# A quarter of a gate softmax moved from matrix products to broadcast rows on three other engines

## The chip, the cores and the metric

One core of a Trainium2 chip runs the whole program; the metric is device time in microseconds, lower is better. The engines are TensorE (PE in the profile, PEld for its weight loads), VectorE (DVE), ScalarE (ACT), GpSimd (POOL) and SyncE (SP), which issues the plain DMAs.

## The reference

Input `x` is (16, 64, 64, 256) in float32: 16 images of 4096 pixels with 256 channels. Four residual layers follow each other, each on the group-normalized (`_gn`) input. Layer 0 adds the nearest of 1024 code vectors, layer 1 an attention of sigmoid scores over rows of 64 pixels, layer 3 a linear attention with a channel norm. The change is in layer 2, a gate from a rank-one softmax over all pairs of pixels of an image:

```python
x = x + _L0_conv_ref(_gn(x), L0_conv_embeddings)      # argmin over 1024 codes, take
x = x + _L1_conv_ref(_gn(x), L1_conv_Wf, ...)
x = x + _L2_conv_ref(_gn(x), L2_conv_w1, ...)
x = x + _L3_conv_ref(_gn(x), L3_conv_w_qkv, ...)

def _L2_conv_ref(x, w1, b1, w2, b2, w3, b3):          # xf: (16, 4096, 256)
    x0 = jnp.einsum('bnc,c->bn', xf, w1) + b1[0]
    x1 = jnp.einsum('bnc,c->bn', xf, w2) + b2[0]
    x2 = jnp.einsum('bnc,c->bn', xf, w3) + b3[0]
    sim = x0[:, :, None] * x1[:, None, :]
    sm = jax.nn.softmax(sim, axis=1)
    feats = jnp.einsum('bn,bnm->bm', x2, sm)
    gate = jax.nn.sigmoid(feats).reshape(b, h, w, 1)
    return gate * x
```

For each column m of 4096 the gate is thus sum over n of x2[n] exp(x0[n] x1[m] - max), divided by the sum of the exponentials alone: 16.8 million exponentials per image.

## The kernel before, in words

The order of work on every engine is written out by hand. `images(B)` runs 15 loop bodies. In one, `new` goes through layers 0 and 1 and the set-up of layer 2, `old` (the image before) through the gate softmax and most of layer 3, and `last` (the one before that) through the end of layer 3 and its output. Each engine has its own list of calls such as `fill(old, 34, 0); score(new, 0, 0)`; a call issues a few instructions with semaphore waits ahead of them. An engine runs its list strictly in order, so a call that waits holds everything behind it. Behind the loop stands a last list, where `old` is the last image and there is no `new`.

The 4096 pixels are 32 tiles of 128. Gate softmax before, on image `old`, in `HALVES = 64` steps h:

- `fill(h, z)`, two matmuls with 12 rows of contraction (x0 and x1 split into bf16 pieces, so that the products come out exact enough), writes sim minus its bound for 128 values of n and 2 x 512 values of m into two PSUM banks, z = 0 or 1. Line 1363.
- `exp(h, z)` on ScalarE: one instruction of 1024 columns, PSUM to one of three SBUF buffers E. Line 601.
- `sums(h)`: four float32 matmuls, each recorded as two, with weights x2 and ones, add the numerators and denominators into PSUM bank 4 over all steps. Line 1372.
- `gate_chain`: the sums are copied, turned by TensorE, divided on VectorE, put through the sigmoid; `spread` and `gating` apply them.

Beside it on the lists stand: `final_z`, `final_sq` and `final_out` (the finish of `last`), `turn_in` (the input of `new` is transposed by TensorE, copied by VectorE), `score(new, t, half)` (six matmuls of 512 columns for half the codes of tile t; banks 5 and 6, one for each half), `best` and `index` (VectorE: maximum and its index, lines 867 and 873), GpSimd's `index` (the indexed load of code rows), `turn0` and `add0` (transpose and add), `l0_norm` and `l1_norm` (ScalarE scales, GpSimd subtracts for the low half), and layers 1 and 3.

The set-up of layer 2 (`project`, `columns`, `extremes`, `pieces`, `piece_turn`) makes x0, x1 and x2 of `new`: as rows in `rows3`, and turned, pixel on the partition, in `s3`.

SBUF is nearly full, so buffers have several uses: `work` holds the biased scores of layer 0, `soft` the q and k of layer 3 and the third E, `o_hi` also the squares of `final_sq`, `yout` the output and the gate sums.

## Time and profile before

| | |
|---|---|
| device time, median of 3 runs (lowest, highest) | 5608.44 us (5603.64, 5612.08) |
| profiled execution, first to last instruction | 5601.4 us |
| profiled execution, its own device time | not recorded; the median lies 7.0 us above its span |
| TensorE busy | 5252.2 us, 94% of the span |
| VectorE busy | 4106.3 us, 73% |
| ScalarE busy | 3978.2 us, 71% |
| GpSimd busy | 1936.0 us, 35% |
| mean granted TensorE clock | 0.966 |

Busy time is the union of an engine's instructions. Those of TensorE and ScalarE overlap at their ends, so the mean length of one is more than what it adds in a row. The granted clock is the share of TensorE's full speed. The chain that ended last follows the work back from the last instruction, at each step to what released it.

### The profile page before, as it was taken

Reading aid. Unit: us, or ns where it says so; the run is one execution under the profiler, and the core shown is the slowest. Engines: PE = TensorE matmul, PEld = TensorE weight load, DVE = VectorE, ACT = ScalarE, POOL = GpSimd, SP = SyncE. Lnnn points to the kernel's source line nnn. Section 1 sums busy time; section 2 is a strip of 40 time slices with the busy share of each in tenths; the row PEclk is TensorE's granted clock in tenths of the full one; section 3 lists DMA queues with packets and bytes.
Section 4 is the critical chain, followed back from the end, with each engine's and each line's share of the span. In section 5 each row is a group of like instructions: output and inputs, shape, how many; then the busy total and the mean of one; then the engine's idle time right before and its main releaser. Section 6 shows DMA issues by size and latency. Waiting matters only on the chain.

```text
span 5601.4 us, 113931 instructions
## 1 busy us (share of the span) xinstructions
PE 5252.2 (94%) x44520; PEld 2737.7 (49%) x44520; DVE 4106.3 (73%) x8674; ACT 3978.2 (71%) x6023; POOL 1936.0 (35%) x1594
## 2 busy tenths in 40 slices
...
GB/s 86 9 37 11 68 25 52 37 6 72 20 61 31 13 67 15 64 28 35 48 11 70 23 57 33 15 64 17 61 31 20 61 13 67 26 47 40 7 31 31
DMA packets 163253, 211.22 MB, mean 38 GB/s; under 512 B 13217, under 2 KB 146081, under 8 KB 162721
## 3 DMA queue, kind: packets, MB, share of 16 engines
...
## 4 chain that ended last, share of the span: by engine, by line
PE 66%; ACT 13%; DVE 11%; issue 6%; POOL 2%; DMA 1%; ACTq 0%; DVEq 0%; SPq 0%; POOLq 0%
PE PS L1195 33%; PE PS L1372 15%; PE PS L1363 6%; ACT n_x L529 3%; DVE stats L849 2%; PE PS L1471 2%; PE PS L1229 2%; PE PS L1253 2%; PE PS L1306 2%; ACT big L601 2%; ACT xin L529 2%; DMA quant_H<-emb_t,idx 1%; ACT work L568 1%; ACT attn L578 1%; ACT soft L601 1%
## 5 line engine op out<-in xcount | busy, mean ns | idle before, releaser
L601 ACT ACTIVATE big<-PS 128x1024 f32<-128x1024 f32 x1376 | 1365.8, 1024 | 460.3 <-PE PS L1363 398.9
L601 ACT ACTIVATE soft<-PS 128x1024 f32<-128x1024 f32 x672 | 676.2, 1024 | 353.9 <-PE PS L1363 346.3
L416 POOL DMA_INDIRECT quant_H<-emb_t,idx x512 | 487.4, 952 | 976.2 <-DVE idx L873 781.2
L1195 PE MATMUL PS<-e_hi,n_hi 128*128 128x512 f16 x2048 | 780.2, 381 | 17.3 <-DVE m L867 9.5
L1195 PE MATMUL PS<-e_hi,n_lo 128*128 128x512 f16 x2048 | 776.7, 379 | 0.0
L1195 PE MATMUL PS<-e_lo,n_hi 128*128 128x512 f16 x2048 | 776.7, 379 | 0.0
L1372 PE MATMUL PS<-big,w 128*4 128x512 f32 x5504 | 756.5, 638 | 0.0
L849 DVE BATCH_NORM_STATS2 stats<-XT 128x6 f32<-128x512 f32 x1024 | 651.7, 683 | 14.5 <-POOL XT L432 4.6
L873 DVE FIND_INDEX8 idx<-m,work 128x8 uint32<-128x1024 f32 x512 | 622.1, 1219 | 0.0
L1363 PE MATMUL PS<-rhs,lhs 12*128 12x512 bf16 x4096 | 557.6, 395 | 61.7 <-ACT big L601 38.8
L867 DVE CUSTOM_DVE_ANT_0 work<-PS,e_bias,m 128x512 f32<-128x512 f32 x512 | 384.0, 750 | 213.2 <-PE PS L1195 189.5
L867 DVE CUSTOM_DVE_ANT_0 work<-PS,e_bias 128x512 f32<-128x512 f32 x512 | 349.1, 682 | 247.1 <-PE PS L1195 239.4
L474 POOL TENSOR_TENSOR rstd<-rstd,mhalf 128x4 f32<-128x4 f32 x128 | 129.2, 1009 | 1106.1 <-DVE rstd L1054 1106.1
L1363 PEld LDWEIGHTS PS<-rhs,lhs 12*128 12x128 bf16 x4096 | 141.7, 91 | 720.2 <-ACT big L601 329.2
L529 ACT ACTIVATE n_x<-XT,gt,gs 128x512 f32<-128x512 f32 x512 | 391.9, 806 | 60.9 <-DVE gt L844 58.4
L409 POOL TENSOR_TENSOR n_lo<-n_x,n_hi 128x1024 f16<-128x1024 f32 x128 | 273.1, 2134 | 399.8 <-ACT n_hi L545 382.3
L1372 PE MATMUL PS<-soft,w 128*4 128x512 f32 x2688 | 379.0, 637 | 16.7 <-ACT soft L601 16.7
L1195 PEld LDWEIGHTS PS<-e_hi,n_hi 128*128 128x128 f16 x2048 | 199.4, 97 | 314.7 <-DVE m L867 69.4
L426 POOL TENSOR_TENSOR n_lo<-n_x,n_hi 128x1024 f16<-128x1024 f32 x128 | 273.4, 2136 | 208.4 <-ACT n_hi L559 155.4
L432 POOL TENSOR_TENSOR XT<-XT,big 128x1024 f32<-128x1024 f32 x128 | 300.2, 2367 | 90.8 <-DVE big L961 90.8
L1065 DVE SCALAR_TENSOR_TENSOR yout<-soft,rstd,PS 128x256 f32<-128x256 f32 x512 | 221.6, 475 | 139.2 <-PE PS L1471 121.1
L1195 PEld LDWEIGHTS PS<-e_hi,n_lo 128*128 128x128 f16 x2048 | 200.4, 98 | 242.2 <-issue 0.6
(208 smaller groups left out, 10799.7 us busy)
## 6 DMA issues: line engine op xcount, KB each, us to landing
xin<-x SPq DMA_DIRECT2D x128, 512.0 KB, 3.9
out<-yout SPq DMA_DIRECT2D x128, 512.0 KB, 2.9
quant_H<-emb_t,idx POOLq DMA_INDIRECT x512
XT<-emb SPq DMA_DIRECT2D x1, 1024.0 KB, 6.2
...
```

The source lines that it names most:

```text
L409: nc.gpsimd.tensor_tensor(n_lo[:, g % 2, :, :], n_x[:, g % 2, :, :], n_hi[:, g % 2, :, :], ALU.subtract).then_inc(l0_lo.sem, 1)
L416: nc.gpsimd.indirect_dma_start(quant[:, g % 2, u, :], None, emb_t, bass.IndirectOffsetOnAxis(ap=idx[:, t % (2 * GT), 0:1], axis=0),).then_ ...
L426: nc.gpsimd.tensor_tensor(n_lo[:, g % 2, :, :], n_x[:, g % 2, :, :], n_hi[:, g % 2, :, :], ALU.subtract).then_inc(l1_lo.sem, 1)
L432: nc.gpsimd.tensor_tensor(here, here, gated[:, g % 2, :, :], ALU.add).then_inc(g_added.sem, 1)
L529: return nc.scalar.activation(dst, XT[:, im % 2, k, g, :], copy, scale=gs[:, layer, k:k + 1], bias=gt[:, layer, k:k + 1])
L601: nc.scalar.activation(E[h % 3][:, z * 1024:(z + 1) * 1024], bank(2 * z, 2), ACT.Exp).then_inc(exped.sem, 1)
L849: last = v.bn_stats(stats[:, layer, k, g, :], XT[:, im % 2, k, g, :])
L867: v.tensor_tensor_reduce(biased[:, t % 2, part], bank(5 + half), e_bias[:, part], 1.0, m8[:, t % 2, 0:1] if half else -BIG, ALU.add, ALU.m ...
L873: v.max_index(idx[:, t % (2 * GT), :], m8[:, t % 2, :], biased[:, t % 2, :]).then_inc(l0_indexed.sem, 1)
L1195: ins = mm(dst, a, b, start=first and j == 0, stop=last and j == 2)
L1363: ins = mm(bank(r), lhs[rr, t * P:(t + 1) * P], rhs[rr, f * GW:(f + 1) * GW], start=True, stop=True)
L1372: ins = mm(PS[32 * q:32 * q + 4, 4, :], w2[:, t, f, :], E[h % 3][:, q * 512:(q + 1) * 512], start=h == 0, stop=h == HALVES - 1, skip_group ...
```

## The change

The 32 tiles of m are split: `NA = 24` stay on the matrix path, `NB = 8` (6 for VectorE, `KD`, and 2 for GpSimd, `KP`) leave it. The matrix path packs its 24 tiles so that each step still fills four banks, which makes 48 steps of 64.

For the other 8 tiles, m lies on the partition and n along the row. `rows_out` stores the rows x0 and x2 to DRAM, `rows_back` loads them into all 128 partitions, 2048 values of n at a time. `bexp` is one ScalarE instruction over 2048 columns, exp(x1[m] * x0[n] - max), with x1 and the negated maximum as per-partition scale and bias, and with the denominator in its accumulator; `bsum` multiplies by x2 and sums on VectorE. `pexp` does 1024 columns, and `pmul` on GpSimd multiplies by x2 and halves the length by additions until 32 are left. `gate_chain` puts the parts together. Buffers are shared anew, with waits for it, and the lists of calls are laid out anew on all engines for the steady loop and the last list. In the loop, the first `score` of `new` stands behind fill 26 (before: fill 34) on TensorE's list, the last `turn_in` behind fill 21 (before: 28).

```diff
-HALVES = 2 * NT
+KD, KP = 6, 2
+NB = KD + KP
+NA = NT - NB
+R1 = (NA - QUADS * GT) // GT
+PER = QUADS // R1
+HALVES = NT + NT // PER
...
+def strip_tiles(h):
+
+    f, i = h // NT, h % NT
+    return f, [i if f == 0 else PER * i + r // R1 for r in range(QUADS)]
...
+    rows_d = nc.dram_tensor("rows_d", (B, 2, NT * P), F32)
...
-        squares = o_hi[:, :, :, :].rearrange("p s k n -> p (s k n)").bitcast(F32).rearrange("p (u c) -> p u c", u=GT)
+        squares = sb("squares", [P, 2, C], BF16)
...
+        x0_rows = [o_both[:, :], soft[:, 0:2048]]
+        x2_rows = [n_both[:, :], o_both[:, :]]
+        EB = [work[:, :], yout[:, :, :, :].rearrange("p s u c -> p (s u c)")]
+        EP = o_x0[:, :, :].rearrange("p k n -> p (k n)")
...
+            def rows_out(im):
+                sp.wait_ge(*rows_kept.after(im, 1))
+                for i in range(2):
+                    sp.dma_start(rows_d[im, i, :].rearrange("(b q n) -> q b n", b=2, q=QUADS),
+                                 rows3[2 * i:P:32, :, :]).then_inc(rows_sent, 16)
+
+            def rows_back(im, c):
+                if c == 0:
+                    sp.wait_ge(rows_sent, 32 * (im + 1))
+                    sp.wait_ge(*rows_turned.after(im, 1))
+                    sp.wait_ge(*pieces_turned.after(im, 0))
+                    if im > 0:
+                        sp.wait_ge(*l3_qved.after(im - 1, NG - 1))
+                        sp.wait_ge(*l3_ked.after(im - 1, NG - 1))
+                else:
+                    if KD > 0:
+                        sp.wait_ge(*b_exped.after(im, KD - 1))
+                    if KP > 0:
+                        sp.wait_ge(*p_exped.after(im, 2 * KP - 1))
+                    if im > 0:
+                        sp.wait_ge(*f_half.after(im - 1, 2 * NG - 1))
+                for i, rows in enumerate((x0_rows, x2_rows)):
+                    sp.dma_start(rows[c], rows_d[im, i, c * 2048:(c + 1) * 2048].partition_broadcast(P)).then_inc(rows_in[c], 16)
...
+            def pmul(im, c, i):
+                n, g = c * KP + i, nc.gpsimd
+                pool.wait_ge(*p_exped.after(im, n))
+                pool.wait_ge(rows_in[c // 2], 32 * (im + 1))
+                pool_chain.link(pool, g.tensor_tensor(EP, EP, x2_rows[c // 2][:, c % 2 * 1024:(c % 2 + 1) * 1024], ALU.mult))
+                w = 512
+                while w > 32:
+                    pool_chain.link(pool, g.tensor_tensor(EP[:, 0:w], EP[:, 0:w], EP[:, w:2 * w], ALU.add))
+                    w //= 2
+                if c == 0:
+                    g.tensor_tensor(pnum[:, i, :], EP[:, 0:32], EP[:, 32:64], ALU.add).then_inc(p_summed.sem, 1)
+                else:
+                    pool_chain.link(pool, g.tensor_tensor(EP[:, 0:32], EP[:, 0:32], EP[:, 32:64], ALU.add))
+                    g.tensor_tensor(pnum[:, i, :], pnum[:, i, :], EP[:, 0:32], ALU.add).then_inc(p_summed.sem, 1)
...
+            def bexp(im, c, i):
+                n, t = c * KD + i, NA + i
+                act.wait_ge(rows_in[c], 32 * (im + 1))
...
+                act.wait_ge(*b_summed.room(im, n, 1))
+                nc.scalar.activation(EB[c], x0_rows[c], ACT.Exp, scale=s3[:, 1, t:t + 1], bias=negm[:, t:t + 1],
+                                     accum_out=bden[:, i, c:c + 1]).then_inc(b_exped.sem, 1)
...
+            def pexp(im, c, i):
...
+                act.wait_ge(*p_summed.room(im, n, 1))
+                nc.scalar.activation(EP, x0_rows[c // 2][:, c % 2 * 1024:(c % 2 + 1) * 1024], ACT.Exp,
+                                     scale=s3[:, 1, t:t + 1], bias=negm[:, t:t + 1],
+                                     accum_out=bden[:, KD + i, c:c + 1]).then_inc(p_exped.sem, 1)
...
+            def bsum(im, c, i):
+                n = c * KD + i
+                dve.wait_ge(*b_exped.after(im, n))
+                dve.wait_ge(rows_in[c], 32 * (im + 1))
+                v.tensor_tensor_reduce(EB[c], EB[c], x2_rows[c], 1.0, 0.0, ALU.mult, ALU.add,
+                                       bnum[:, i, c:c + 1]).then_inc(b_summed.sem, 1)
...
             def fill(im, h, z):
-                f, t = h // NT, h % NT
+                f, tiles = strip_tiles(h)
...
-                    ins = mm(bank(r), lhs[rr, t * P:(t + 1) * P], rhs[rr, f * GW:(f + 1) * GW], start=True, stop=True)
+                    ins = mm(bank(r), lhs[rr, tiles[r] * P:(tiles[r] + 1) * P], rhs[rr, f * GW:(f + 1) * GW], start=True, stop=True)
```

Further edits, not shown: `gate_chain` on VectorE adds the parts (11 short operations for 5), `pieces` copies in 6 more pieces, `extremes` also makes `negm`, and ScalarE, VectorE, SP and TensorE wait for the last reader of a shared buffer before it is written again.

## Rows read from the trace of the kernel before

**Rows 1.** Windows: us, busy PE, PEld, DVE, ACT, POOL, granted clock, DMA share, GB/s.

```profile
2614.60:2703.20 88.60, 84.51 (x673) 34.19 (x674) 56.96 (x130) 79.80 (x139) 10.89 (x10) 0.94 0.29 96
2703.20:2824.00 120.80, 120.69 (x724) 48.83 (x720) 97.94 (x213) 67.45 (x80) 43.52 (x37) 1.00 0.11 34
2824.00:2841.00 17.00, 14.67 (x100) 3.61 (x98) 7.66 (x21) 13.39 (x15) 3.36 (x4) 0.90 0.06 17
2841.00:2952.50 111.50, 103.79 (x1291) 83.03 (x1292) 93.10 (x179) 87.60 (x144) 62.53 (x49) 1.00 0.01 2
```

**Rows 2.** The view of source line 927: durations in ns, first and last start in us.

```profile
L927 DVE TENSOR_REDUCE mt<-PS x16: 278/279/280, 236.1 to 5295.5; 2x1 f32<-2x128 f32 x16
```

**Rows 3.** The chain that ended last, in time: start us, us, what.

```profile
2733.41 2.69 PE PS L1372 x24
...
2751.58 5.29 PE PS L1195 x24
...
2780.58 0.59 PE PS L1253 x4
...
2785.48 0.97 PE PS L1372 x8
```

**Rows 4.** Timeline around the start of stage A: start us, us, engine, line, operation.

```profile
2611.44 0.27 PE L1195 MATMUL PS<-qv_hi,o_lo 128*128 128x256 f16 x1
...
2614.98 3.77 ACT L601 ACTIVATE big<-PS 128x1024 f32<-128x1024 f32 x4
...
2619.98 0.61 PE L1363 MATMUL PS<-rhs,lhs 12*128 12x512 bf16 x4
...
2621.55 1.02 ACT L601 ACTIVATE big<-PS 128x1024 f32<-128x1024 f32 x1
...
2622.59 0.39 PE L1363 MATMUL PS<-rhs,lhs 12*128 12x512 bf16 x2
2623.02 2.87 ACT L601 ACTIVATE big<-PS 128x1024 f32<-128x1024 f32 x3
```

**Rows 5.** Groups by line and form, ScalarE out of SBUF: busy us, mean ns.

```profile
L529 ACT ACTIVATE n_x<-XT,gt,gs 128x512 f32<-128x512 f32 x512 | 391.9, 806 | 60.9 <-DVE gt L844 58.4
...
L545 ACT ACTIVATE n_hi<-n_x 128x512 f16<-128x512 f32 x256 | 148.3, 622 | 224.1 <-PE PS L1195 221.1
...
L667 ACT ACTIVATION_READ_ACCUMULATOR o_hi<-PS 128x1 f32 x512 | 106.5, 208 | 0.0
...
L520 ACT ACTIVATE e_hi<-XT 128x2048 f16<-128x2048 f32 x1 | 1.9, 1911 | 0.0
```

**Rows 6.** Groups of VectorE by line and form.

```profile
L867 DVE CUSTOM_DVE_ANT_0 work<-PS,e_bias 128x512 f32<-128x512 f32 x512 | 349.1, 682 | 247.1 <-PE PS L1195 239.4 <-DVE idx L873 3.0 <-issue 2.4
...
L867 DVE DVE_READ_ACCUMULATOR2_ANT m<- 128x1 f32 x1024 | 84.7, 83 | 0.0
...
L952 DVE TENSOR_TENSOR gate<-PS,nums 128x16 f32<-128x16 f32 x32 | 4.1, 169 | 0.5
```

**Rows 7.** Timeline: a two-input VectorE operation that meets one of GpSimd.

```profile
2568.83 2.13 POOL L437 TENSOR_TENSOR o_lo<-o_x,o_hi 128x1024 f16<-128x1024 f32 x1 [6.11 <-ACT o_hi L633]
...
2570.32 1.19 DVE L979 TENSOR_TENSOR soft<-soft,qsum 128x512 f32<-128x512 f32 x1
```

**Rows 8.** Groups of GpSimd by line and form.

```profile
L432 POOL TENSOR_TENSOR XT<-XT,big 128x1024 f32<-128x1024 f32 x128 | 300.2, 2367 | 90.8 <-DVE big L961 90.8
...
L453 POOL TENSOR_TENSOR r<-s,pk 128x96 f32<-128x96 f32 x16 | 5.8, 366 | 1.3
```

**Rows 9.** DMA issues: size, median us to landing.

```profile
XT<-emb SPq DMA_DIRECT2D x1, 1024.0 KB, 6.2
```

**Rows 10.** Timeline of the tail: the last gather, then layer 1's first product.

```profile
2828.30 0.94 POOL L416 DMA_INDIRECT quant_H<-emb_t,idx  x1 [3.02 <-DVE idx L873]
...
2842.48 0.29 PE L1272 MATMUL PS<-n_hi,fg_hi 128*32 128x256 f16 x4 [0.25 <-issue]
```

**Rows 11.** Windows: gate softmax of the last image.

```profile
5324.20:5469.40 145.20, 134.55 (x971) 37.07 (x971) 35.70 (x89) 135.19 (x199) 8.07 (x8) 0.93 0.09 30
```

More of the change, by code:

```diff
@@ L620, in gated @@
                 act.wait_ge(*g_gated.room(im, g, 2))
+                if g == 0 and KP > 0:
+                    act.wait_ge(*p_summed.after(im, 4 * KP - 1))
                 for k in range(KC):
@@ new lines, in _ @@
+                bexp(old, 0, 4); final_sq(last, 14); exp(old, 17, 1); pexp(old, 1, 1); final_sq(last, 15)
+                exp(old, 18, 0); exp(old, 18, 1); exp(old, 19, 0); exp(old, 19, 1); bexp(old, 0, 5)
+                exp(old, 20, 0); exp(old, 20, 1); exp(old, 21, 0); exp(old, 21, 1); exp(old, 22, 0)
+                exp(old, 22, 1); exp(old, 23, 0); exp(old, 23, 1); l0_norm(new, 0, 0); l0_norm(new, 0, 1)
+                exp(old, 24, 0); l0_norm(new, 0, 2); l0_norm(new, 0, 3); exp(old, 24, 1); exp(old, 25, 0)
@@ L863, in best @@
                     dve.wait_ge(*l0_indexed.room(im, t, 2))
+                    if t == 0 and im > 0 and KD > 0:
+                        dve.wait_ge(*b_summed.after(im - 1, KD - 1))
                 else:
@@ new lines, in _ @@
+                final_z(last, 2); fill(old, 6, 0); fill(old, 6, 1); sums(old, 4); final_z(last, 3)
+                final_out(last, 1); sums(old, 5); fill(old, 7, 0); fill(old, 7, 1); turn_in(new, 0)
+                final_z(last, 4); final_out(last, 2); sums(old, 6); final_out(last, 3); fill(old, 8, 0)
+                fill(old, 8, 1); turn_in(new, 1); final_z(last, 5); final_out(last, 4); fill(old, 9, 0)
+                fill(old, 9, 1); turn_in(new, 2); sums(old, 7); final_z(last, 6); fill(old, 10, 0)
@@ new lines, in _ @@
+                fill(old, 10, 1); sums(old, 8); sums(old, 9); fill(old, 11, 0); turn_in(new, 3)
+                final_z(last, 7); final_out(last, 5); fill(old, 11, 1); fill(old, 12, 0); turn_in(new, 4)
+                sums(old, 10); final_z(last, 8); final_out(last, 6); turn_in(new, 5); fill(old, 12, 1)
+                fill(old, 13, 0); sums(old, 11); final_z(last, 9); final_out(last, 7); fill(old, 13, 1)
+                sums(old, 12); fill(old, 14, 0); final_z(last, 10); fill(old, 14, 1); turn_in(new, 6)
@@ new lines, in _ @@
+                turn_in(new, 12); sums(old, 16); final_out(last, 13); fill(old, 18, 1); fill(old, 19, 0)
+                fill(old, 19, 1); final_out(last, 14); turn_in(new, 13); fill(old, 20, 0); sums(old, 17)
+                fill(old, 20, 1); final_out(last, 15); sums(old, 18); turn_in(new, 14); fill(old, 21, 0)
+                turn_in(new, 15); fill(old, 21, 1); sums(old, 19); fill(old, 22, 0); fill(old, 22, 1)
+                sums(old, 20); gn(new, 0, 1); fill(old, 23, 0); fill(old, 23, 1); gn(new, 0, 2)
@@ new lines, in _ @@
+                fill(old, 24, 0); sums(old, 21); sums(old, 22); fill(old, 24, 1); fill(old, 25, 0)
+                sums(old, 23); sums(old, 24); fill(old, 25, 1); fill(old, 26, 0); score(new, 0, 0)
+                score(new, 0, 1); score(new, 1, 0); score(new, 1, 1); score(new, 2, 0); fill(old, 26, 1)
+                fill(old, 27, 0); score(new, 2, 1); score(new, 3, 0); score(new, 3, 1); fill(old, 27, 1)
+                score(new, 4, 0); score(new, 4, 1); fill(old, 28, 0); fill(old, 28, 1); sums(old, 25)
@@ new lines, in _ @@
+                sums(old, 26); turn0(new, 0); score(new, 5, 0); score(new, 5, 1); score(new, 6, 0)
+                sums(old, 27); sums(old, 28); fill(old, 29, 0); fill(old, 29, 1); score(new, 6, 1)
+                score(new, 7, 0); score(new, 7, 1); turn0(new, 1); score(new, 8, 0); score(new, 8, 1)
+                score(new, 9, 0); fill(old, 30, 0); fill(old, 30, 1); score(new, 9, 1); score(new, 10, 0)
+                turn0(new, 2); fill(old, 31, 0); fill(old, 31, 1); sums(old, 29); sums(old, 30); turn0(new, 3)
@@ new lines, in _ @@
+                fill(old, 34, 1); fill(old, 35, 0); score(new, 18, 1); turn0(new, 6); score(new, 19, 0)
+                score(new, 19, 1); turn0(new, 7); score(new, 20, 0); score(new, 20, 1); sums(old, 33)
+                sums(old, 34); fill(old, 35, 1); fill(old, 36, 0); score(new, 21, 0); score(new, 21, 1)
+                turn0(new, 8); fill(old, 36, 1); fill(old, 37, 0); score(new, 22, 0); score(new, 22, 1)
+                turn0(new, 9); score(new, 23, 0); fill(old, 37, 1); fill(old, 38, 0); sums(old, 35)
@@ new lines, in _ @@
+                sums(old, 36); sums(old, 37); fill(old, 38, 1); fill(old, 39, 0); score(new, 23, 1)
+                score(new, 24, 0); score(new, 24, 1); fill(old, 39, 1); fill(old, 40, 0); score(new, 25, 0)
+                score(new, 25, 1); turn0(new, 10); score(new, 26, 0); fill(old, 40, 1); fill(old, 41, 0)
+                sums(old, 38); sums(old, 39); sums(old, 40); fill(old, 41, 1); fill(old, 42, 0)
+                score(new, 26, 1); score(new, 27, 0); turn0(new, 11); score(new, 27, 1); score(new, 28, 0)
```

897 lines of the change are left out of this document (412 added, 485 removed).

## The prediction

> **What bounds the kernel now.** First the times of the stages. One image after another goes through the steady loop, and one tiny instruction per image (L927) marks the period: 15 periods lie between its first and its last start, (5295.5 − 236.1)/15 = 337.3 us each, with 236.1 us ahead and 305.9 us behind [rows 2]. Then busy time by stage of one period [rows 1], cut where the work changes: A (88.6 us), the gate softmax beside the finish of the image before; B (120.8 us), the softmax beside the 64 score halves of the next image; its tail (17.0 us), from the last score to the gate sums; C (111.5 us), layers 1 and 3. The reader is to see that each has another limit. In B TensorE is busy 120.69 of 120.8 us, VectorE only 97.94. In A TensorE has 84.51 but ScalarE 79.80 of 88.6. In C no engine passes 93%.
>
> A busy TensorE may be only waiting for ends, so I add B up from the chain [rows 3]. 24 score matmuls last 5.29 us, 0.216 each once overlapped; a turn of a gathered pair 0.59 us; one `sums` step 0.97 us alone and (2.69 − 0.97)/2 = 0.86 in a row. One half-fill (two matmuls) is 0.61 − 0.39 = 0.22 us [rows 4]. B's order holds 384 score matmuls, 13 turns, 48 half-fills and 23 sums: 82.9 + 7.7 + 10.6 + 19.8 = 121.0 us, and B lasts 120.8. So B is TensorE's stream with no slack. The tail is a latency chain: the last gather is issued at 2828.30 and layer 1's first product waits until 2842.48 [rows 10]; work taken from TensorE there gains nothing.
>
> **The change, part by part.** Sums go by this profile's span, 5601.4 us; the median of the runs shown is 7.0 us more, and I carry that over.
>
> 1. *TensorE loses a quarter of the softmax.* The steps fall from 64 to 48 an image: 32 half-fills and 16 sums less, 7.0 + 13.8 = 20.8 us. The new orders split it. Before the first score A issued 69 half-fills and 33 sums, now 53 and 25: −10.4 us. B proper goes from 48 and 23 to 35 and 16: 112.1 us in place of 121.0, −8.9. The rest is in the tail and hidden.
>
> 2. *ScalarE does as many exponentials, at more each.* 32 exponentials of 1024 columns out of PSUM go; a queued one costs (3.77 − 1.02)/3 = 0.92 us [rows 4]. In come 12 of 2048 columns (`bexp`) and 8 of 1024 (`pexp`) from SBUF, with pointer scale, pointer bias and an accumulator read. 2048 plain columns take 1.91; pointers add 0.80 − 0.62 = 0.18 at 512 columns; the read is 0.20 to 0.21 [rows 5]. With 0.1 of overlap (1.02 against 0.92) `bexp` is 2.2 us against 1.84 for two old ones, +0.36. `pexp` is 1.05 (between 0.62 and 1.91) + 0.18 + 0.21 − 0.1 = 1.34 against 0.92, +0.42. That is 12 × 0.36 + 8 × 0.42 = 7.7 us an image; bounds 3.5 (the read hidden) and 10 (no overlap). Half falls in A, whose exponential count is otherwise the same (16 equivalents replace 16): ScalarE's floor in A becomes 79.8 + 3.8 = 83.6 us. In B it had 67 of 121 us and 3.9 more are hidden. The Trainium skill ("ScalarE: Activation LUTs", "What ACT_TABLE_LOAD costs") gives 186 ns + 0.833 ns a column and 93 ns for each pointer operand; two pointers make 0.19 us where the rows have 0.18, and a `bexp` by it is an estimated 2.08 us before the read and 0.1 less of overlap, which leaves my sum as it is.
>
> 3. *VectorE gets 12 multiply-and-sum passes over 2048 columns (`bsum`).* No such length is in the trace. The nearest: 512 columns with an accumulator, 0.682 us, and its read 0.083 [rows 6]. 512 columns at 0.96 a ns are 0.533, so 0.15 is fixed and 2048 take 2.28 + 0.08 = 2.37 us. As bounds: all of 0.682 in proportion, 2.73 + 0.08; the bare columns, 2.13. Six lie in A, five in B proper, one behind B's statistics in the tail, where VectorE is busy 7.66 of 17 us. A: 57.0 + 14.2 = 71 us, no limit. B: two statistics and an add move into the tail (three operations of 0.65, −2.0), so 97.9 − 2.0 + 11.9 = 107.8 us.
>
> 4. *`bsum` reads two SBUF tensors while GpSimd works.* The one operation that does this now, L979, is as long as others of 512 columns are, 0.68 us [rows 6], where it meets none of GpSimd's work, but 1.19 when it starts 0.64 us before the end of a GpSimd subtraction that began at 2568.83 and lasts 2.13: it ends 0.55 us, about its bare columns, after that one does [rows 7]. So it waits out the other engine. A `bsum` loses nothing if it meets none, and at most a 2.4 us multiplication; I take 0.5 us, so VectorE in B is at 110.3. The Trainium skill ("SBUF — State Buffer", "SBUF: two separate sides") calls the pair of ports an exclusive lock held for a whole instruction, and that speaks against this change, which puts two-input work on both engines; the row agrees. The reverse holds too: a GpSimd subtraction that meets a `bsum` starts up to 2.3 us late, and score matmuls follow it.
>
> 5. *GpSimd gets 8 multiply-and-halve chains.* 1024 columns are 2.37 us, 96 are 0.37 [rows 8]: 0.16 + 2.16 ns a column. The lengths 1024, 512, 256, 128, 64, 32 sum to 5.3 us, 5.5 with a second short add: 44 us an image, four chains in A and four in B. GpSimd goes from 43.5 to 66 of 121 us in B and stays off the limit, but a gather queued behind a chain comes up to 5.5 us late. The turns that need it are also placed later (turns 5 and 6 behind score 16 and 18, where 14 and 16 stood), so I charge nothing; uncovered, it would be 5.5 us for four chains.
>
> 6. *Row loads.* Two 1 MB broadcasts go out when the last layer-3 product is done, 2611.7; the first `pexp` comes after eight exponentials and a copy, at 2623.02 + 1.0 + 0.6 = 2624.6 [rows 4]. 12.9 us are there. A 1 MB load landed after 6.2 us [rows 9]; two at full overlap or none take 6.2 to 12.4. Hidden. The next input loads queue behind them on SP, but the first turn of them sits behind fill 7, over 20 us on. The second pair goes out after the last finish of A; twelve exponentials and eight normalizations, some 17 us of ScalarE, stand between that and its first reader. Hidden, narrowly.
>
> 7. *Small things.* The gate chain has 11 short VectorE operations for 5 at 0.17 us [rows 6], the pieces 6 more short copies, and `negm` one more: +1.0 us in C at most, partly covered; I take 0.8.
>
> **The sum.** A: ScalarE's floor is 83.6, and today its idle time there is 8.8 us, in a stage where TensorE is as full. With 10 us off TensorE, and exponentials that need no fill, I leave 3.4: 87.0. The granted clock is 0.94 in A and 0.93 in the last image's softmax [rows 1, 11], where ScalarE sets the pace as it will in A, so I charge nothing for it. B: the floors are 112.1 (TensorE) and 110.3 (VectorE). Today one is full with the other at 81%; at 98% both can't be, since each score half needs a free bank from VectorE and TensorE's in-order queue stops. I take 4% on the larger: 116.5. Tail 17.0. C 111.5 + 0.8 = 112.3. The period is 332.8 for 337.9, −5.1. Fifteen make −76. The last image (A and B merged) is ScalarE's today, 135.19 of 145.20 us [rows 11]: +7.7, less about 5 of its 10 idle, +3; the first and last chains +1. 5601.4 − 76 + 4 = 5529, and 7 for the median: **5536 us**, 1.3% faster.
>
> **Rivals.**
> - *The orders pack as well as now.* B at TensorE's 112.1, A at 84.5, C unchanged: 325.1, −12.8 × 15 = −192, so 5420 us. For it: B has no loss today, and indexing is put off by a half so that banks come free sooner. Against: VectorE has 19% of air today and would have 2%.
> - *VectorE takes over B* (the other side). If each `bsum` waits a whole GpSimd operation (2.1) and VectorE keeps a fifth of the 22.9 us that it now idles there, B is 107.8 + 10.7 + 4.6 = 123; A is then late too, 88.6, and C 113: 341.6, +3.7 × 15 = +56, so 5668 us. It decides from B at 121.6, the value at which my other stages add up to 337.9. For it: the overlap of [rows 7] and the GpSimd load doubled in A; against: only a part of GpSimd's time in B is tensor work, 0.94 us an indexed load being gathers.
> - *The rows come late.* Every load time over 12.9 us stops ScalarE, and behind it all fills. At 17 us, under half the rate of the row shown, 4 us a period: 5596 us. Against: [rows 9].
> - *ScalarE's added time is on the path beyond A*, in the sense that the upper bound of step 2 holds and A packs no better than now, 79.8 + 5 + 8.8 = 93.6: period 339.4, +22 + 4, so 5635 us.
>
> **How the numbers follow.** Forecast 0.50, well packed 0.20, VectorE bound 0.13, late rows 0.07, ScalarE 0.10. This kernel's measurement tells 0.2% (11 us) from no change. Faster: 0.50 × 0.96 + 0.20 + 0.07 × 0.6 = 0.72; within 0.2%: 0.06; slower 0.22. Range: 5405 (below the well packed) to 5625 (short of the ScalarE and VectorE cases) leaves out about 0.2; the forecast's own range is 5470 to 5590 (B's loss between 1% and 8%, A's idle time 1.5 to 6).
>
> **What would show it.** Right: 48 steps an image; `bexp` near 2.3 us, `bsum` near 2.4 with a tail of longer ones; ScalarE the fullest in A, over 94%; TensorE and VectorE both over 90% in B; C unchanged. The prediction fails if A stays at 88 us or more (ScalarE's waits then name what is late), if scores wait on L867's successor for over 8 us in B, or if `bsum` is far from 2.4 us.

## The result, and the profile after

The changed kernel takes **5758.48 us** (median of 4 runs, 5756.14 to 5770.8) where the kernel before took 5609.35 beside it (5603.64 to 5612.08): a ratio of 1.0278, interval 1.0266 to 1.029. It is 2.8% slower; forecast were 5536 us and 1.3% faster, and the range ended at 5625. The profiled execution spans 5754.3 us for 5601.4.

Stage times of each kernel are cut in its trace as in [rows 1]: A from the first fill to the first score, B to the last score's end, the tail to the copy of the gate sums, C to the next first fill. (B's end is set 0.2 us behind the last score's own end, in both kernels alike.) They are summed over the 15 periods; ahead of the first fill lie 249.6 and 249.8 us.

| us | before | after | difference | forecast of it |
|---|---|---|---|---|
| A, 15 | 1327.6 | 1462.4 | +134.8 | −24 |
| B, 15 | 1821.3 | 1773.8 | −47.5 | −65 |
| tail, 15 | 249.4 | 235.5 | −13.9 | 0 |
| C, 15 | 1676.3 | 1743.5 | +67.2 | +12 |
| last image, A and B | 145.2 | 162.7 | +17.5 | +3 |
| behind it | 132.0 | 126.6 | −5.4 | 0 |

The source line that answers to [rows 2], with the same columns:

```profile
L1031 DVE TENSOR_REDUCE mt<-PS x16: 278/278/279, 235.4 to 5433.8; 2x1 f32<-2x128 f32 x16
```

(5433.8 − 235.4)/15 = 346.6 us a period, 9.3 more than before. B became shorter, as it should; A and C ate it. Windows of one period of the changed kernel (A, B, tail, C) and of the last image's softmax; columns as in [rows 1]:

```profile
2667.00:2765.50 98.50, 81.86 (x582) 35.22 (x583) 73.88 (x141) 82.64 (x145) 42.47 (x36) 0.88 0.37 124
2765.50:2882.70 117.20, 112.67 (x638) 46.78 (x638) 106.02 (x221) 73.04 (x89) 73.04 (x65) 1.00 0.12 34
2882.70:2898.00 15.30, 12.10 (x86) 3.27 (x84) 11.66 (x26) 10.33 (x12) 3.08 (x4) 0.89 0.08 24
2898.00:3014.00 116.00, 104.98 (x1287) 83.56 (x1287) 98.86 (x187) 86.00 (x142) 63.73 (x55) 0.99 0.02 5
5465.00:5627.70 162.70, 130.56 (x779) 36.17 (x779) 65.58 (x112) 139.06 (x204) 64.12 (x59) 0.76 0.14 50
```

Against [rows 1] and [rows 11]: TensorE in B is at 112.67, forecast 112.1; VectorE at 106.02, forecast 110.3; ScalarE in A at 82.64, forecast 83.6. None of the three floors was exceeded by more than 0.6 us. But A lasts 98.5 us and no engine in it passes 84%: the time goes into waiting in a ring, in which each engine's next operation needs the result of another's. The granted clock fell too, from 0.94 to 0.88 in A and from 0.93 to 0.76 in the last image (a mean of its two levels, 1 for 2.4 GHz and 0.5 for 1.2).

Groups by line and form, of the lines that answer to [rows 5, 6, 8] (mean ns after the comma):

```profile
L1076 DVE CUSTOM_DVE_ANT_0 work<-work,n_both 128x2048 f32<-128x2048 f32 x96 | 279.9, 2916 | 14.6 <-ACT work L688 14.6
...
L1076 DVE CUSTOM_DVE_ANT_0 yout<-yout,o_both 128x2048 f32<-128x2048 f32 x96 | 237.1, 2470 | 48.6 <-ACT yout L688 48.6
L535 POOL TENSOR_TENSOR o_x<-o_x 128x512 f32<-128x512 f32 x128 | 222.7, 1740 | 10.0
L1187 DVE SCALAR_TENSOR_TENSOR yout<-soft,rstd,PS 128x256 f32<-128x256 f32 x512 | 221.6, 475 | 111.3 <-PE PS L1599 57.6 <-POOL rstd L525 53.7
L688 ACT ACTIVATE work<-o_both,negm,s 128x2048 f32<-128x2048 f32 x96 | 202.1, 2105 | 3.9 <-DVE bnum L1076 3.9
...
L525 POOL TENSOR_TENSOR rstd<-rstd,mhalf 128x4 f32<-128x4 f32 x128 | 186.8, 1460 | 899.3 <-DVE rstd L1176 899.3
...
L532 POOL TENSOR_TENSOR o_x<-o_x,n_both 128x1024 f32<-128x1024 f32 x64 | 176.5, 2758 | 35.6 <-ACT o_x L699 35.6
...
L699 ACT ACTIVATE o_x<-o_both,negm,s 128x1024 f32<-128x1024 f32 x64 | 79.6, 1245 | 2.6 <-POOL pnum L538 2.6
...
L688 ACT ACTIVATION_READ_ACCUMULATOR work<-o_both,negm,s 128x1 f32 x96 | 19.8, 207 | 0.0
```

The first row block's sums (`work`, in A) are 2.92 us in the mean, the second's 2.47. GpSimd's products of 1024 columns are 2.76 on the first row block where the same length took 2.37 [rows 8], and its power of −0.5 on four columns, L525, has 1.46. Why, the timeline in A shows:

```profile
2687.18 0.69 DVE L1173 TENSOR_TENSOR soft<-PS,gamma_b 128x512 f32<-128x512 f32 x1 [2.46 <-ACT squares L770]
2687.79 0.16 DVE L1176 TENSOR_SCALAR rstd<-sq 128x4 f32<-128x4 f32 x1
2687.86 2.28 DVE L1076 CUSTOM_DVE_ANT_0 work<-work,n_both 128x2048 f32<-128x2048 f32 x1
...
2688.03 3.00 POOL L525 TENSOR_TENSOR rstd<-rstd,mhalf 128x4 f32<-128x4 f32 x1 [32.16 <-DVE rstd L1176]
...
2690.98 2.38 POOL L532 TENSOR_TENSOR o_x<-o_x,n_both 128x1024 f32<-128x1024 f32 x1
...
2691.06 0.87 DVE L1187 SCALAR_TENSOR_TENSOR yout<-soft,rstd,PS 128x256 f32<-128x256 f32 x2 [0.31 <-POOL rstd L525]
```

VectorE's `bsum` stands right behind the operation that sends GpSimd its power. The power starts 0.17 us after the sum and ends at 2691.03, 0.89 us after the sum's end (2690.14). The other way round, 25 us on, first GpSimd, then VectorE:

```profile
2712.93 2.35 POOL L532 TENSOR_TENSOR o_x<-o_x,n_both 128x1024 f32<-128x1024 f32 x1
```

```profile
2713.16 4.27 DVE L1076 CUSTOM_DVE_ANT_0 work<-work,n_both 128x2048 f32<-128x2048 f32 x1
```

GpSimd's product ends at 2715.28, and the sum ends at 2717.43, 2.15 us later, about its bare columns: it waited out the product, as L979 did in [rows 7]. Who is late then, in the table of waits in A, 2667.0 to 2765.5 (us, times, longest):

```profile
PEld PS L1323 <- DVE soft L1173: 12.2, 8, 3.0
...
PE PS L1323 <- DVE soft L1173: 7.3, 6, 2.1
```

TensorE waits for VectorE's L1173, which empties the one bank of the last convolution (`final_sq`), and which shares VectorE's queue with the sums. The same wait over the whole run, before (there L1195 for L1051) and after:

```profile
PE PS L1195 <- DVE soft L1051: 4.9, 17, 0.6
```

```profile
PE PS L1323 <- DVE soft L1173: 94.0, 86, 2.1
```

Rows and B's stream: the loads that answer to [rows 9] (1,024 KB, us to landing), and the score and sum steps of the chain that answer to [rows 3]:

```profile
o_both<-rows_d SPq DMA_DIRECT2D x32, 1024.0 KB, 6.7
n_both<-rows_d SPq DMA_DIRECT2D x16, 1024.0 KB, 6.9
soft<-rows_d SPq DMA_DIRECT2D x16, 1024.0 KB, 5.7
```

```profile
2824.57 5.18 PE PS L1323 x24
...
2848.95 2.69 PE PS L1500 x24
```

No engine waits for a row. And 24 score matmuls and 24 of the sums cost what they did. The tail, the stretch of [rows 10], is 15.7 us a period in the mean for 16.6.

### The profile page after: what moved, and what is told of

It reads as the page before. It is cut to its first block, busy times and chain, and to the rows that moved or that the text cites. A ratio compares the mean times of both kernels' runs of the same rounds, so it can differ in the third digit from the quotient of the medians.

```text
span 5754.3 us, 110100 instructions
## 1 busy us (share of the span) xinstructions
PE 5085.6 (88%) x41448; PEld 2721.6 (47%) x41448; DVE 4655.5 (81%) x9171; ACT 4040.9 (70%) x6151; POOL 2921.1 (51%) x2554
## 4 chain that ended last, share of the span: by engine, by line
PE 43%; DVE 19%; issue 18%; ACT 11%; POOL 6%; DMA 2%; SPq 0%; DVEq 0%; ACTq 0%; POOLq 0%
PE PS L1323 24%; PE PS L1500 6%; DVE stats L951 3%; PE PS L1491 3%; DVE work L971 3%; DVE idx L977 2%; PE PS L1434 2%; PE PS L1381 2%; DMA quant_H<-emb_t,idx 1%; ACT big L675 1%; PE PS L1357 1%; ACT o_x L598 1%; PE PS L1599 1%; ACT n_x L598 1%; ACT xin L598 1%
## 5 line engine op out<-in xcount | busy, mean ns | idle before, releaser
L1323 PE MATMUL PS<-e_hi,n_both 128*128 128x512 f16 x4096 | 1304.2, 382 | 77.9 <-DVE m L971 38.4
L675 ACT ACTIVATE big<-PS 128x1024 f32<-128x1024 f32 x1024 | 1012.7, 1026 | 475.5 <-PE PS L1491 472.6
L1323 PE MATMUL PS<-e_lo,n_both 128*128 128x512 f16 x2048 | 780.9, 381 | 0.0
L1323 PEld LDWEIGHTS PS<-e_hi,n_both 128*128 128x128 f16 x4096 | 401.2, 98 | 620.7 <-DVE m L971 121.7
L675 ACT ACTIVATE soft<-PS 128x1024 f32<-128x1024 f32 x512 | 507.9, 1023 | 202.9 <-PE PS L1491 142.8
L525 POOL TENSOR_TENSOR rstd<-rstd,mhalf 128x4 f32<-128x4 f32 x128 | 186.8, 1460 | 899.3 <-DVE rstd L1176 899.3
L1500 PE MATMUL PS<-big,w 128*4 128x512 f32 x4096 | 597.3, 679 | 7.9 <-ACT big L675 7.9
L971 DVE CUSTOM_DVE_ANT_0 work<-PS,e_bias 128x512 f32<-128x512 f32 x512 | 350.9, 685 | 177.5 <-PE PS L1323 172.3
L535 POOL TENSOR_TENSOR o_x<-o_x 128x512 f32<-128x512 f32 (+3 forms) x512 | 456.4, 891 | 40.1
L460 POOL TENSOR_TENSOR n_both<-n_x,n_both 128x1024 f16<-128x1024 f32 x128 | 273.7, 2139 | 275.0 <-ACT n_both L619 273.8
L971 DVE CUSTOM_DVE_ANT_0 work<-PS,e_bias,m 128x512 f32<-128x512 f32 x512 | 378.4, 739 | 32.0 <-PE PS L1323 29.2
L1323 PE MATMUL PS<-h_hi,n_both 128*128 128x256 f16 x2048 | 360.9, 273 | 15.0 <-DVE XT L999 14.8
L477 POOL TENSOR_TENSOR n_both<-n_x,n_both 128x1024 f16<-128x1024 f32 x128 | 273.3, 2135 | 190.3 <-PE PS L1323 97.8
L1323 PE MATMUL PS<-qv_hi,o_both 128*128 128x256 f16 x2048 | 359.0, 274 | 7.4 <-DVE soft L1117 7.4
```

Source lines behind the costliest of these rows:

```text
L460: nc.gpsimd.tensor_tensor(n_lo[:, g % 2, :, :], n_x[:, g % 2, :, :], n_hi[:, g % 2, :, :], ALU.subtract).then_inc(l0_lo.sem, 1)
L535: pool_chain.link(pool, g.tensor_tensor(EP[:, 0:w], EP[:, 0:w], EP[:, w:2 * w], ALU.add))
L675: nc.scalar.activation(E[h % 3][:, z * 1024:(z + 1) * 1024], bank(2 * z, 2), ACT.Exp).then_inc(exped.sem, 1)
L971: v.tensor_tensor_reduce(biased[:, t % 2, part], bank(5 + half), e_bias[:, part], 1.0, m8[:, t % 2, 0:1] if half else -BIG, ALU.add, ALU.m ...
L1323: ins = mm(dst, a, b, start=first and j == 0, stop=last and j == 2)
L1500: ins = mm(PS[32 * q:32 * q + 4, 4, :], w2[:, tiles[q], f, :], E[h % 3][:, q * 512:(q + 1) * 512], start=h == 0, stop=h == HALVES - 1, ski ...
```

## The experiments

Each kernel is the changed one with one edit, or with edits of others put together, timed beside the kernel before (5602 to 5606 us). e1 to e5, e12 and e14 leave out a part of the computation, so they price terms and are no versions to use. Stage times are means per period, of A over the 14 periods that have all three images, of the others over 15: 89.2, 121.4, 16.6 and 111.8 before, **99.2, 118.3, 15.7 and 116.2** after (A, B, tail, C).

| run | us | ratio (interval) | A | B | C | last image |
|---|---|---|---|---|---|---|
| e1 no chain on GpSimd | 5553.07 | 0.9903 (0.9886 to 0.9919) | 89.7 | 113.5 | 116.5 | 156.6 |
| e2 no sums on VectorE | 5579.04 | 0.9953 (0.9936 to 0.997) | 90.1 | 114.8 | 116.2 | 158.8 |
| e3 neither | 5533.54 | 0.9869 (0.9852 to 0.9885) | 90.0 | 112.5 | 116.1 | 156.7 |
| e4 nor the exponentials | 5464.97 | 0.975 (0.9734 to 0.9767) | 86.2 | 112.3 | 116.3 | 144.9 |
| e5 sums of one input | 5580.13 | 0.9966 (0.9952 to 0.9981) | 90.0 | 114.9 | 116.1 | 159.0 |
| e6 chains first | 5707.68 | 1.0184 (1.0167 to 1.0201) | 95.8 | 117.9 | 116.3 | 162.6 |
| e7 all on VectorE | 5783.15 | 1.0316 (1.0299 to 1.0333) | 101.8 | 117.6 | 116.4 | 166.6 |
| e8 old order of C | 5700.42 | 1.0167 (1.015 to 1.0184) | 99.2 | 118.1 | 113.0 | 162.4 |
| e9 two sums earlier | 5747.89 | 1.0252 (1.0235 to 1.0269) | 100.1 | 116.8 | 116.2 | 166.0 |
| e10 e6 and e9 | 5732.0 | 1.0224 (1.0207 to 1.0241) | 98.3 | 117.7 | 116.3 | 165.9 |
| e11 e10 and e8 | 5664.21 | 1.0106 (1.0089 to 1.0123) | 97.6 | 117.0 | 112.7 | 166.2 |
| e12 e11 and e5 | 5573.72 | 0.9941 (0.9924 to 0.9958) | 94.7 | 114.3 | 112.5 | 156.8 |
| e13 e6 and e8 | 5643.59 | 1.0068 (1.0051 to 1.0085) | 95.5 | 117.4 | 112.6 | 166.3 |
| e14 e5 and e8 | 5513.27 | 0.9839 (0.9823 to 0.9855) | 90.3 | 114.2 | 112.5 | 156.8 |
| e15 products on GpSimd | 5771.44 | 1.0295 (1.0276 to 1.0313) | 104.2 | 118.2 | 112.4 | 162.8 |

**Take work away (e1 to e4).** e1 leaves of GpSimd's chain only a last short add:

```diff
-                pool_chain.link(pool, g.tensor_tensor(EP, EP, x2_rows[...][...], ALU.mult))
-                w = 512
...
+                g.tensor_tensor(pnum[:, i, :], EP[:, 0:32], EP[:, 32:64], ALU.add).then_inc(p_summed.sem, 1)
```

> The changed kernel, but each GpSimd chain is only its last 32-column addition; the numerators of 2 tiles are left out. The changed kernel takes 5758 us. Theory 1 (VectorE's passes hold up the finish of the image before in stage A): VectorE's list is unchanged, A stays at 96 us or more, 5700 to 5740 us. Theory 2 (GpSimd's chains stand ahead of the powers that final_out needs, and hold the shared ports): A falls by 6 us or more a period, 5650 us or less. Theory 3 (the new orders or ScalarE's added time cost it by themselves): under 30 us of change.

e2 shortens VectorE's sums, e3 does both:

```diff
-                v.tensor_tensor_reduce(EB[c], EB[c], x2_rows[c], 1.0, ...
+                v.tensor_tensor_reduce(EB[c][:, 0:16], EB[c][:, 0:16], x2_rows[c][:, 0:16], 1.0, ...
```

> The changed kernel, but each VectorE pass covers 16 of 2048 columns; the numerators of 6 tiles are left out. Theory 1: A comes down to 89 us or less, and the last image loses most of its 17 us, so 5550 us or less. Theory 2: A stays at 95 us or more, 5660 us or more, of which B and the tail give some. Theory 3: over 5700 us.

> The changed kernel with both sets of numerators left out as in the two kernels before; exponentials, orders and row loads stay. Theories 1 and 2 both let the orders themselves pay: A near ScalarE's 84 to 88 us and B near 113, 5400 to 5480 us, and the two single effects add up or overlap. Theory 3: 5650 us or more.

e4 also cuts `bexp` and `pexp` to 64 columns, with a scale of 0:

```diff
-                nc.scalar.activation(EB[c], x0_rows[c], ACT.Exp, scale=s3[:, 1, t:t + 1], ...
+                nc.scalar.activation(EB[c][:, 0:64], x0_rows[c][:, 0:64], ACT.Exp, scale=0.0, ...
```

> As the kernel before, and the 20 new exponentials an image cover 64 columns of constants; all of 8 tiles' gate is left out. It is the time of the matrix path's 24 tiles with the new orders: if ScalarE sets A without VectorE's and GpSimd's passes, A falls to 80 us or less, and the kernel by 80 to 150 us below the one with neither set of numerators. If the order alone sets A (theory 3), it changes by less than 30 us.

e1 gains 205 us, e2 179, and both together 225. If each had a cost of its own, e3 would gain 384. So the sums without the chains cost 20 us (e1 to e3), the chains without the sums 46 (e2 to e3), and the other 159 need both: VectorE's sums meeting GpSimd's chains, not either by its length. C is 116 in all four.

e4 takes the new exponentials out whole, not only what they take more than the old ones. Windows of an A and of the last image in e3, then in e4:

```profile
2577.10:2667.20 90.10, 79.32 (x581) 33.03 (x581) 57.23 (x141) 81.91 (x144) 11.83 (x14) 0.91 0.40 135
5259.90:5416.60 156.70, 125.37 (x779) 35.12 (x779) 37.27 (x112) 138.47 (x205) 10.02 (x16) 0.78 0.15 52
```

```profile
2545.60:2631.10 85.50, 76.95 (x582) 32.83 (x583) 57.00 (x141) 68.33 (x145) 11.85 (x14) 0.92 0.41 142
5189.70:5334.60 144.90, 115.74 (x779) 34.26 (x779) 37.44 (x112) 109.66 (x204) 10.05 (x16) 0.85 0.16 55
```

ScalarE loses 13.6 us of work in A and 28.8 in the last image, but A is only 3.8 us shorter in the mean and the last image 11.8. The run gains 69 us on e3; 80 to 150 were expected if ScalarE set A, under 30 if the order alone did. So ScalarE's load alone does not set the length of A.

**The exclusion by itself (e5).** The multiplication by x2 is left out, the length kept. With it goes the second input from SBUF, and also the 2048 columns that the sum writes back (the form below writes one column):

```diff
-                v.tensor_tensor_reduce(EB[c], EB[c], x2_rows[c], 1.0, 0.0, ALU.mult, ALU.add,
-                                       bnum[:, i, c:c + 1]).then_inc(b_summed.sem, 1)
+                v.tensor_reduce(bnum[:, i, c:c + 1], EB[c], AX, ALU.add).then_inc(b_summed.sem, 1)
```

> Each numerator on VectorE is a plain sum of the 2048 exponentials (one input) instead of the sum of products with x2 (two inputs); the multiplication is left out, everything else stays, GpSimd's chains too. If VectorE and GpSimd wait for each other over a shared port whenever VectorE has two inputs in SBUF, this removes the exclusion and keeps the occupancy: the sums are never stretched over 2.5 us, the powers on GpSimd stay near 1.01 us, the first part of the period comes to 89 to 92 us as with either engine's work taken out, and the time to 5560 to 5620. If it is only that 2.3 us on VectorE's queue and 5.5 us on GpSimd's stand ahead of the last convolution's work, nothing changes: first part 98 to 101 us, time 5720 to 5770.

The time falls by 178 us though a sum is as long as before. It is the time of e2, where the sums have almost no length (5580 and 5579): what they cost there is not their place in VectorE's queue. Groups by form in e5:

```profile
L1076 DVE TENSOR_REDUCE bnum<-work 128x1 f32<-128x2048 f32 x96 | 218.9, 2280 | 14.6 <-ACT work L688 14.6
```

```profile
L535 POOL TENSOR_TENSOR o_x<-o_x 128x512 f32<-128x512 f32 x128 | 163.4, 1276 | 10.0
L532 POOL TENSOR_TENSOR o_x<-o_x,n_both 128x1024 f32<-128x1024 f32 x64 | 151.7, 2371 | 43.5 <-ACT o_x L699 43.5
...
L525 POOL TENSOR_TENSOR rstd<-rstd,mhalf 128x4 f32<-128x4 f32 x128 | 129.7, 1013 | 883.5 <-DVE rstd L1175 883.5
```

The sum has the same 2.28 us that a two-input one has alone, but none is stretched; the product is back at 2.37, the add of 512 columns at 1.28 for 1.74, the power at 1.01 for 1.46. Timeline of e5, first VectorE, then GpSimd:

```profile
2611.86 2.28 DVE L1076 TENSOR_REDUCE bnum<-work 128x1 f32<-128x2048 f32 x1
```

```profile
2612.03 1.03 POOL L525 TENSOR_TENSOR rstd<-rstd,mhalf 128x4 f32<-128x4 f32 x1 [32.14 <-DVE rstd L1175]
2613.01 2.38 POOL L532 TENSOR_TENSOR o_x<-o_x,n_both 128x1024 f32<-128x1024 f32 x1
```

The same three operations as at 2687.86 above, and now they overlap. TensorE's wait for `final_sq` over the run is down from 94.0 us, to about what it is in e1 (35.5) and e2 (34.7):

```profile
PE PS L1322 <- DVE soft L1172: 37.0, 75, 0.8
```

Is it the second input, or the columns written? VectorE's L971 in the changed kernel tells: it too writes SBUF, 512 columns, but only one of its two inputs is in SBUF, the other in PSUM. 375 of its 1024 executions overlap one of GpSimd's tensor operations, and none is stretched (ns, least, median, most; the other 512, which take one value more, have 725/734/752):

```profile
L971 DVE CUSTOM_DVE_ANT_0 work<-PS,e_bias x512: 667/691/694, 44.8 to 5331.1; 128x512 f32<-128x512 f32 x171
```

So writing SBUF alone does not make VectorE wait. The operations that wait each other out are those with two inputs in SBUF on VectorE, and GpSimd's; the Trainium skill ("SBUF — State Buffer", "SBUF: two separate sides") has this as a lock held for a whole instruction, and e5 agrees.

**Is it the order? (e6, e9, e10).** e6 moves GpSimd's first two chains each ahead of a power:

```diff
-                final_sq(last, 1); pmul(old, 0, 0); final_sq(last, 3); final_sq(last, 5); final_sq(last, 7)
-                pmul(old, 0, 1); final_sq(last, 9); ...
+                pmul(old, 0, 0); final_sq(last, 1); final_sq(last, 3); final_sq(last, 5); pmul(old, 0, 1)
+                final_sq(last, 7); final_sq(last, 9); ...
```

> Only GpSimd's order changes: in each steady period its first chain stands ahead of the first power of -0.5 instead of behind it, and its second one place earlier too, so that each chain falls into a time in which GpSimd idles. If the chains hurt by standing ahead of a due power in GpSimd's queue, the first part falls from 98 to 101 us to 91 to 95 us and the time to 5640 to 5700. If it is the port, the chain only meets other VectorE work there and little is gained: 97 to 100 us, time 5730 to 5770.

−51 us, nearly all of it in A (99.2 to 95.8): 22 us under what the exclusion alone allowed, 8 us over what the queue alone did, and about a third of the loss. e9 moves VectorE's first two sums ahead of the operation that sends the power:

```diff
-                ... final_sq(last, 0); final_sq(last, 1); bsum(old, 0, 0)
+                ... final_sq(last, 0); bsum(old, 0, 0); final_sq(last, 1)
```

> Only VectorE's order changes: the first two numerators of a period stand ahead of the operation that sends GpSimd its power of -0.5, instead of right behind it, so that sum and power no longer meet. If the cost in the first part is the meeting (powers of 3.0 us instead of 1.0 and what waits for them): the two long powers of a period are gone, the first part 95 to 98 us instead of 98 to 101, time 5690 to 5730. If it is GpSimd's chain ahead of the second power in its queue: no gain, 5740 to 5770.

> Both orders: VectorE's first two sums ahead of the power's operands, and GpSimd's first chains ahead of the due powers. The chain alone gave 5708. If the port's exclusion is the rest of it, the two together give 92 to 95 us in the first part and 5650 to 5690; if the two edits remove the same wait, it stays at 5700 to 5715.

e9: 5747.89 us, ratio 1.0252 (1.0235 to 1.0269). e10: 5732.0, 1.0224 (1.0207 to 1.0241), *slower* than e6 by 24, and outside both of its expectations. The powers in e9:

```profile
L525 POOL TENSOR_TENSOR rstd<-rstd,mhalf 128x4 f32<-128x4 f32 x128 | 131.6, 1028 | 975.4 <-DVE rstd L1176 975.4
```

All but one of the long powers are gone, and A is no shorter (100.1 us in the mean). A sum ahead of `final_sq` delays the convolution's bank: TensorE waits 139.2 us for it over the run, for 94.0. So e9 changes two things and doesn't price the long powers. e1 does, for a kernel without chains: its powers are 1.48 us in the mean, and A is 89.7. What they cost beside the chains isn't shown.

**All numerators on VectorE (e7).** 16 sums of 2048 columns an image, GpSimd without chains:

```diff
-KD, KP = 6, 2
+KD, KP = 8, 0
```

> All 8 row tiles go to VectorE (16 sums of products of 2048 an image instead of 12) and GpSimd has no chain; ScalarE's exponentials are the same in columns (16 of 2048 instead of 12 of 2048 and 8 of 1024). If what costs is the meeting of VectorE's and GpSimd's added work, this does better than the changed kernel although VectorE has 9 us an image more: first part 90 to 93 us, middle part 115 to 118, time 5570 to 5640. If VectorE's own load is what costs, the time is 5780 or more (VectorE is busy 106 of 117 us in the middle part already).

(With it go new lists, with places for the added sums.) Slower than the change, at 5783: A 101.8 us, B 117.6 with VectorE at 109.6 in it. Neither expectation held as a whole; VectorE's added load was nearer. In e7 ScalarE also waits 204.9 us for the sums to free its buffers (40.7 in the changed kernel), which may come of the places that I gave the new ones. So e7 says only that dropping the chains isn't enough when their work goes to VectorE as two-input sums.

**C's order (e8).** The lists of all four engines from the gate on as the kernel before has them; on ScalarE for example (line breaks moved):

```diff
-                gate_chain(old, 1); l1_fg(new, 0); l1_norm(new, 2); l1_tanh(new, 0); gated(old, 2)
-                l1_fg(new, 1); l1_norm(new, 3); l1_tanh(new, 1); gated(old, 3); ...
+                gate_chain(old, 1); l1_fg(new, 0); l1_norm(new, 2); gated(old, 2); l1_tanh(new, 0)
+                l1_fg(new, 1); l1_norm(new, 3); l1_tanh(new, 1); gated(old, 3); gated(old, 4); ...
```

> The last part of each period (from the copy of the accumulators to the next first fill) issues in the order that the kernel before has, on all four engines; the rest is as changed. It was 111.6 us before and is 116.5 us in the changed kernel and in the four experiments so far. If the new order makes the difference: 111 to 113 us there, time 5670 to 5700. If it is work that the change adds there (six more copies ahead of the fills, the rows' buffers), the part stays at 116 to 117 and the time at 5740 to 5770.

C falls from 116.2 to 113.0 us and the time by 58, at the edge of what was expected if the order does it; window of one C of e8:

```profile
2881.80:2995.50 113.70, 104.41 (x1290) 84.11 (x1287) 94.83 (x186) 86.41 (x143) 64.00 (x55) 0.98 0.02 7
```

The same work is done in 2.3 us less here (116.00 in the window of the changed kernel above), 3.2 in the mean.

**Together (e11 to e14).** e11 is e10 with e8's lists, e12 is e11 with e5's sums, e13 is e6 with e8's lists, e14 is e5 with them.

> As the run before it, with the last part of the period in the order of the kernel before (which alone gave 58 us). If these are independent: 58 us under the run before it, 5590 to 5640, about what the kernel before takes (5603).

> As the run before it, with VectorE's sums of one input (the multiplication by x2 left out), so that no sum holds the port. What it takes less than the run before it is what the exclusion still costs in the best order tried: if it is the middle part's 3 us and the first part's rest, 5500 to 5540 against 5590 to 5640; if the new orders have already taken the meetings away, the two come out within 20 us.

> GpSimd's chains ahead of the due powers (5708 alone) and the last part of the period in the order of the kernel before (58 us alone), VectorE's sums where the change has them. If the two gains add: 5640 to 5660, under the 5664 of the version that also moved VectorE's sums. If moving the sums was of use: 5680 or more.

> Sums of one input where the change has them (5580 alone) with the last part in the old order. If moving the sums is what cost 5 us a period in the last run, and the old order of the last part gives its 58 us here too: 5510 to 5530, 50 us under the run with moved sums. If the gain of the last part's order is given back in the next first part whatever the place of the sums: 5565 to 5580.

e12 took 5573.72 us (0.9941, 0.9924 to 0.9958), 90 us less than e11: in these orders too the exclusion costs, and more than the 20 us of its second expectation. Even without the exclusion the moved sums (and GpSimd's chains, moved with them) cost 60 us against e14, where they stand as the change has them. e11 gained 68 us on e10, e13 64 on e6, e14 67 on e5: C's order is independent of the rest. e13 is the fastest that leaves nothing out, 5643.59 us, still 0.7% slower than before; e14 estimates what the change would take if VectorE's sums never held GpSimd up, 5513.27. Windows of A, B, C and the last image in e14:

```profile
2560.00:2649.90 89.90, 79.62 (x582) 32.95 (x583) 69.17 (x136) 82.10 (x144) 32.95 (x36) 0.91 0.41 136
2649.90:2764.70 114.80, 113.00 (x642) 47.11 (x638) 104.86 (x215) 73.09 (x88) 66.30 (x65) 0.99 0.12 34
2781.70:2894.10 112.40, 103.01 (x1289) 82.61 (x1289) 94.86 (x186) 86.56 (x142) 62.95 (x55) 1.00 0.02 9
5222.30:5379.10 156.80, 124.06 (x779) 34.74 (x779) 62.32 (x101) 138.52 (x204) 51.76 (x60) 0.79 0.14 50
```

**Can the exclusion be kept out? (e15).** On e13, five of the six sums of the first block become a product on GpSimd and a one-input sum on VectorE:

```diff
+            def bmul(im, c, i):
...
+                nc.gpsimd.tensor_tensor(EB[0], EB[0], x2_rows[0], ALU.mult).then_inc(b_mulled.sem, 1)
...
+                    v.tensor_reduce(bnum[:, i, c:c + 1], EB[c], AX, ALU.add).then_inc(b_summed.sem, 1)
```

> As e13, but 5 of the 6 numerators in the first part are split: GpSimd multiplies all 2048 columns, VectorE sums them with one input (for these no sum holds the port; the second row block stays as it was, and the last image too). GpSimd gets 5 times about 4.6 us (twice the 2.3 of its product of 1024 columns) in the first part, where it is busy some 40 of 96 us. If the exclusion is the cost there and GpSimd has the room: first part 91 to 93 us instead of 95 to 96, time 5580 to 5610. If the longer products stand ahead of the powers as the chains did: first part 98 us or more, time 5680 or more.

5771: A 104.2 us. GpSimd's timeline there:

```profile
2726.07 1.02 POOL L526 TENSOR_TENSOR rstd<-rstd,mhalf 128x4 f32<-128x4 f32 x1
2727.06 4.54 POOL L532 TENSOR_TENSOR work<-work,n_both 128x2048 f32<-128x2048 f32 x1
```

On the first row block next to nothing is stretched (powers 1.03 us in the mean, products of 1024 columns 2.36), but 4.54 us stand in GpSimd's queue five times a period, and its 56 busy us of 102 leave little room ahead of each power: over the run TensorE waits 128.4 us for `final_sq`, for 58.7 in e13. The exclusion was traded for a queue.

## Why the prediction was wrong

**The step that failed is step 4**, and step 5's "GpSimd stays off the limit" with it. Step 4 saw the exclusion in [rows 7], named the reverse direction too, and then entered it in the sum as 0.5 us of VectorE's time for each of the five sums in B alone. The size was about right (2.69 us in the mean of all sums for 2.28 alone, 0.41 more), the place was not. In A it went in as nothing, because A was costed by engine totals: ScalarE's floor plus some idle time. A is a ring, from the convolution's single bank over `final_sq` on ScalarE and VectorE, the power on GpSimd and `final_out` back to TensorE. The sums alone leave it at 89.7 us (e1), the chains alone at 90.1 (e2), both without the exclusion at 90.0 (e5); both with it make 99.2. Removing the exclusion alone gives 178 us (e5), 9.2 a period in A and 3.3 in B; with C's order put back it is 130 to e13 and 187 to e8 (5700.42 − 5513.27).

A second term had been put at nothing, the new order of C (step 7 below). The kernel is 222 us over the forecast: 178 are the exclusion, 67 more go with C's old order (e5 to e14), and e14 is 23 under the forecast.

How the 9.2 us of A split is only partly settled. The sums' own stretching is 6 × 0.64 = 3.8 us (2.92 against 2.28), if all of it is on the path; moving the chains in GpSimd's queue gives back 3.4 (e6), and that overlaps with the exclusion, since the chains' place costs nothing without it (e5). What the long powers cost, and what the rest is, stays open.

The other steps:
1. *TensorE, −20.8.* Right: B's stream was forecast at 112.1, TensorE is busy 112.67, and e4 runs B in 112.3.
2. *ScalarE.* Durations right (`bexp` 2.1 + 0.2 less overlap, forecast 2.2; `pexp` 1.24 + 0.2 for 1.34), but what they add is half of the forecast: ScalarE is busy 4040.9 us for 3978.2, 3.9 an image more for 7.7. The model of A, this floor plus a little idle time, was wrong even without sums and chains: e4 runs A in 86.2 us with ScalarE at 68.33. The last image was mis-sized: it is 11.6 longer without the exclusion (156.8 in e14 for 145.2), forecast 3, though ScalarE is busy only 3.3 more in it.
3. *`bsum`, 2.28 + 0.08.* Right to the hundredth when nothing meets it.
5. *Chains.* 5.3 to 5.5 us forecast; the means without exclusion in e5 are 2.37 + 1.28 + 0.73 + 0.46 + 0.32 + 0.25 = 5.4. With it 2.76 + 1.74 + 0.76 + 0.71 + 0.35 + 0.25 = 6.6. That they delay nothing was wrong, but the delay needs the sums too (e5).
6. *Rows.* Right: 5.7 to 6.9 us, no wait.
7. *C, +0.8.* The work was right: C is 112.6 with the old lists (e13), 111.8 before. The new lists cost 3.6 more, and these I had put at nothing: I took "orders laid out anew" as good as the old ones in a stage that the change does not otherwise touch. The diff had them in full.

The clock was charged nothing. It fell from 0.94 to 0.88 in A and to 0.76 in the last image. It is low also where the exclusion is gone (0.91 and 0.79 in e14), and 0.92 and 0.85 where the new exponentials are cut short (e4). No run holds it apart from ScalarE's pace, so what it costs isn't shown; it may be a part of the 11.6.

Of the rivals, the well packed case, the late rows and ScalarE's upper bound did not come. "VectorE takes over B" had the right mechanism at the wrong stage: B stayed at 118.3, under its point of decision of 121.6, while A went to 99.2, over the 88.6 that it gave A. Without the exclusion and with C's old order the total comes near, and a part of that is luck: e14 measured 5513, the forecast was 5536, but A is 90.3 for 87.0 and the last image 156.8 for 148.2, and B at 114.2 for 116.5 makes up for both; C is 112.5 for 112.3.
